# Relation rows of a graph network kernel: another split of their building over the stages

## What is computed

```python
edge_index = jnp.stack([src, dst])
x = x + _L0_gnn_ref(_layernorm(x), edge_index, ...)      # 3 mean-aggregation layers
x = x + _L0_ffn_ref(_layernorm(x)[None], ...)[0]         # 16 experts, the best 2 for each node
x = x + _L1_gnn_ref(_layernorm(x), edge_index, edge_type_500, ...)
x = x + _L1_ffn_ref(_layernorm(x)[None], ...)[0]         # 8 experts, the best 2 for each node
```

```python
h_src = h_hc[src]
r_uv = r_hc[edge_type]
m = clifford_linear(h_src * r_uv, msg_w, msg_b)
gate = jax.nn.sigmoid(r_uv.reshape(r_uv.shape[0], -1) @ gate_w.T + gate_b)
m = m * gate[:, :, None]
```

## Time and profile before

| what | value |
| --- | --- |
| median of three executions | 3093.87 us |
| the profiled execution | 3092.59 us |
| its span, first to last instruction | 3091.0 us |
| mean granted TensorE clock | 0.915 of full speed |
| TensorE matmul busy | 2442.2 us (79%) |
| VectorE busy | 1786.1 us (58%) |
| GpSimd busy | 1742.3 us (56%) |
| ScalarE busy | 1450.7 us (47%) |
| moved by DMA | 516.56 MB, 167 GB/s in the mean |

### The profile page before, as it was taken

How to read it: one execution, slowest core, us unless ns; L and a number is a source line. 1 busy time by engine, 2 the same in 40 slices (tenths; PEclk the granted TensorE clock), 3 DMA queues, 4 the chain that set the end, 5 groups by cost and what they waited for, 6 DMA issues and landing times. The chain is left out here.

```text
span 3091.0 us, 52879 instructions
## 1 busy us (share of the span) xinstructions
PE 2442.2 (79%) x14195; PEld 1910.2 (62%) x14195; DVE 1786.1 (58%) x5132; ACT 1450.7 (47%) x3766; POOL 1742.3 (56%) x1702
## 2 busy tenths in 40 slices
PE   1759999969999489850877777787877775899997
PEld 0336666747777478750655555555555554799996
DVE  7669889747788521037776666666666666311110
ACT  0357666535565333333644444444444433455553
POOL 1647777667774045422777777777777750233332
PEclk9989999989999589985998999988898987899998
DMA  6748777578886233543666666666666643443232
GB/s 226 253 143 233 227 209 211 168 227 257 263 251 186 85 109 103 168 128 125 197 186 185 180 186 184 182 182 187 181 187 185 190 119 101 121 106 77 49 65 64
DMA packets 289373, 516.56 MB, mean 167 GB/s; under 512 B 79344, under 2 KB 137057, under 8 KB 287084
## 3 DMA queue, kind: packets, MB, share of 16 engines
q0 software_dynamic: 86192, 225.20, 28.2%
q1 hardware_dynamic: 185532, 267.85, 26.4%
q10 hardware_dynamic: 17392, 20.46, 2.0%
HBM read 381.08 MB, written 137.11 MB: 168 GB/s over the span
## 5 line engine op out<-in xcount | busy, mean ns | idle before, releaser
L726 POOL DMA_INDIRECT agg_r_rows<-h_table,parts_and_x x832 | 831.0, 999 | 336.9 <-issue 230.1
L817 PE MATMUL agg_r_sums<-agg_r_rows,agg_r_onehot 128*128 128x257 f32 x1664 | 489.4, 422 | 259.9 <-DVE agg_r_rows L798 171.8
L817 PEld LDWEIGHTS agg_r_sums<-agg_r_rows,agg_r_onehot 128*128 128x128 f32 x1664 | 305.4, 203 | 396.3 <-issue 318.0
L686 ACT ACTIVATE agg_r_gap<-iota,parts_and_x 128x128 f32<-128x128 f32 x832 | 286.6, 392 | 449.8 <-PE agg_r_sums L817 419.8
L780 DVE TENSOR_TENSOR acc<-acc,agg_r_sums 128x257 f32 (+1 forms) x834 | 351.9, 422 | 129.1 <-PE agg_r_sums L817 44.9
L1723 POOL DMA_INDIRECT rl_buf<-r_table,kinds x304 | 327.6, 1078 | 150.0 <-issue 78.9
L2119 PEld LDWEIGHTS f_pH<-f_xT,f_w 128*128 128x128 f32 x2816 | 332.3, 195 | 40.0 <-ACT f_xT L2197 17.9
L2119 PE MATMUL f_pH<-f_xT,f_w 128*128 128x128 f32 x2816 | 346.7, 280 | 9.9 <-ACT f_xT L2197 4.5
L831 PE MATMUL agg_r_spread<-xn 128*128 128x257 bf16 x2664 | 350.2, 292 | 0.0
L1526 PE MATMUL la_acc<-la_parts,la_counts 128*128 128x512 f32 x1250 | 309.1, 404 | 29.3 <-DVE la_parts L1633 29.3
L2138 PE MATMUL f_pY<-f_w,f_hT 128*128 128x256 f32 x1408 | 325.6, 381 | 7.5 <-DMA f_w<-in_L_ffn_w 7.5
(11 more groups left out here) (418 smaller groups left out, 3596.8 us busy)
## 6 DMA issues: line engine op xcount, KB each, us to landing
agg_r_rel<-relation_rows SPq DMA_DIRECT2D x305, 260.0 KB, 3.0
relation_rows<-rl_buf SPq DMA_DIRECT2D x152, 260.0 KB
relation_rows<-rm_buf SPq DMA_DIRECT2D x125, 260.0 KB, 3.3
agg_r_rows<-h_table,parts_and_x POOLq DMA_INDIRECT x832, 3.2
f_w<-in_L_ffn_W SPq DMA_DIRECT2D x18, 512.0 KB, 5.4
f_w<-in_L_ffn_W SPq DMA_DIRECT2D x9, 1024.0 KB, 4.8
f_w<-in_L_ffn_w SPq DMA_DIRECT2D x30, 256.0 KB, 3.1
f_w<-in_L_ffn_w SPq DMA_DIRECT2D x15, 512.0 KB, 3.6
```

The source lines that it names most:

```text
L686: last = nc.scalar.activation(gap[:, n % HOT, t, :], c.iota[:, 0:P], ACT.Abs, bias=c.tab["b_near"][:, column(g) + t:column(g) + t + 1])
L726: pool.indirect_dma_start(rows[:, n % SLOTS, t, :], None, table, bass.IndirectOffsetOnAxis(ap=indices[:, t:t + 1], axis=0)).then_inc(s_row ...
L817: last = nc.tensor.matmul(sums[:, (2 * n + t) % BANKS, 0:used], onehot[:, n % HOT, t, :], rows[:, n % SLOTS, t, 0:used], start=True, stop= ...
```

## The change

28, 152 and 125 pairs become 18, 136, 135 and 16 pairs. The last 16 are new beside the first router's scoring: `norm_and_gate` gets a `RelationRows` with a ring of eight pairs. There GpSimd issues the gathers of eight pairs, clears the semaphores and issues the other eight; SyncE stores two or three pairs ahead of each of the five row stores and three behind them, and waits for all. In `gnn0_start` SyncE stores four pairs, then four (before: seven), then two ahead of each product store (before: three) and none behind. All 305 pairs are built as before, and nothing else is changed.

```diff
--- before.py
+++ after.py
@@ -79,7 +79,7 @@
         ORDER.append(("extra", (_n + 1) // EXTRA_EVERY - 1))
 MADE = [n for n in range(BLOCKS) if n >= FIRST_MADE and (n - FIRST_MADE) % MADE_EVERY == 0]
 STORED = [n for n in range(BLOCKS) if n not in MADE]
-SHARES = (56, 304, 250)
+SHARES = (36, 272, 270, 32)
 assert sum(SHARES) == 2 * len(STORED) and len(ORDER) == BLOCKS + EDGES_AT // 2
 GW = 3 * D + 2
 CHUNK = 5
@@ -839,7 +839,7 @@
                     beside.tensor(pe, n)
 
 
-def norm_and_gate(nc, c, name, ne, gate, gate_bias, logits, xn_table, update=None, tables=()):
+def norm_and_gate(nc, c, name, ne, gate, gate_bias, logits, xn_table, update=None, tables=(), relation=None):
 
     PRODUCTS, LATE = 3, 2 * J
     with Core(nc) as k:
@@ -855,6 +855,7 @@
             a_turns, product = k.ps(f"{name}_a_turns", [P, 2, 512]), k.ps(f"{name}_product", [P, PRODUCTS, 512])
             s_at, s_aT, s_product, s_used = (k.sem(f"{name}_{x}") for x in ("at", "aT", "product", "used"))
         s_tables = k.sem(f"{name}_tables_in")
+        work = RelationRows(nc, c, k, f"{name}_r", *relation, ring=8) if relation else None
         with nc.Block() as block:
 
             @block.sync
@@ -862,9 +863,14 @@
                 for out, src in tables:
                     sp.dma_start(out, src).then_inc(s_tables, 16)
                 for i in range(NJ):
+                    if work:
+                        work.store(sp, work.pairs * i // (NJ + 1), work.pairs * (i + 1) // (NJ + 1))
                     sp.wait_ge(s_xn, (i + 1) * J)
                     sp.dma_start(xn_table[i * J * P:(i + 1) * J * P, :].rearrange("(t p) d -> p t d", p=P), c.xn[:, i * J:(i + 1) * J, :])\
                         .then_inc(s_table, 16)
+                if work:
+                    work.store(sp, work.pairs * NJ // (NJ + 1), work.pairs)
+                    work.stored(sp)
                 sp.wait_ge(s_table, 16 * NJ)
                 if tables:
                     sp.wait_ge(s_tables, 16 * len(tables))
@@ -988,7 +994,11 @@
 
             @block.gpsimd
             def _(pool):
+                if work:
+                    work.fetch(pool, 0, work.RING)
                 Core.clear(pool)
+                if work:
+                    work.fetch(pool, work.RING, work.pairs)
 
 
 def row(ap):
@@ -1174,7 +1184,7 @@
                     sp.dma_start(out, src, allow_slow_non_contiguous=True).then_inc(s_more[q // 6], 16)
                 work.store(sp, 0, 4)
                 eb.save_starts(sp)
-                work.store(sp, 4, 11)
+                work.store(sp, 4, 8)
                 sp.wait_ge(s_norm, NT)
                 sp.dma_start(z[:, D:2 * D].rearrange("(t p) d -> p t d", p=P), h[:, :, :]).then_inc(s_saved, 16)
                 sp.wait_ge(s_w, 4)
@@ -1182,7 +1192,7 @@
                     sp.dma_start(folded[l - 1, :, 0:4 * D], f.w[:, l, :, :].rearrange("p k n -> p (k n)")).then_inc(s_saved, 16)
                     sp.dma_start(folded[l - 1, :, 4 * D:5 * D], f.shift[:, l, :]).then_inc(s_saved, 16)
                 for b in range(NJ):
-                    work.store(sp, 11 + 3 * b, 14 + 3 * b)
+                    work.store(sp, 8 + 2 * b, 10 + 2 * b)
                     sp.wait_ge(s_z0, (b + 1) * J)
                     sp.dma_start(z[b * J * P:(b + 1) * J * P, 0:D].rearrange("(t p) d -> p t d", p=P), f.z[:, b * J:(b + 1) * J, :])\
                         .then_inc(s_saved, 16)
@@ -1190,7 +1200,7 @@
                         eb.save_blocks(sp)
                     if b == 3:
                         eb.save_groups(sp)
-                work.store(sp, 11 + 3 * NJ, work.pairs)
+                work.store(sp, 8 + 2 * NJ, work.pairs)
                 sp.wait_ge(s_saved, 16 * (5 + NJ))
                 work.stored(sp)
                 eb.saved(sp)
@@ -2784,7 +2794,8 @@
         xn_table = c.dram("xn_table", [NP, D])
         norm_and_gate(nc, c, "ng0", E0, *c.gates[0], logits[0], xn_table, None,
                       [(c.tab[n][:, :], c.tab[n + "_d"]) for n in ("b_src", "b_near", "b_start")]
-                      + [(c.tab["b_tile"][:, 2 * LAG:HALVES + 2 * LAG], c.tab["b_tile_d"])])
+                      + [(c.tab["b_tile"][:, 2 * LAG:HALVES + 2 * LAG], c.tab["b_tile_d"])],
+                      (r_table, relation_rows, sum(SHARES[:3]), SHARES[3]))
 
         c.h = c.sb("h1", [P, NT, D])
         c.h_rstd, c.h_down = c.sb("h1_rstd", [P, NT]), c.sb("h1_down", [P, NT])
```

## The result

The kernel after takes 3070.38 us in the median of four executions (3063.36 to 3073.00), the kernel before on the same chip 3096.91 (3089.11 to 3101.50): ratio 0.9922, 95% interval 0.9905 to 0.9940. Its profiled execution took 3068.61 us with a span of 3067.0.

A forecast was written before the change was run, and what follows sets the result against it. Relation rows were taken to end the first dense product and count matrix, arithmetic layers 1 and 2. The terms -8.7 - 16.5 + 4.9 + 9.5 = -10.8 us gave 3083 us, with an 8-in-10 range of 3075 to 3090.

The forecast's parts named there:

- What bounds the kernel: Relation rows end the first dense product and count matrix (some 17 us late); arithmetic ends layers 1 and 2, leaving about 25 us free.
- 5.42 us: Time from the end of the last store's issue to the next stage's first instruction, taken from the count matrix's end.
- First dense product: 10 pairs fewer there: next stage's first instruction at 158.4 against 167.12, -8.7 us (ends -8, -10).
- 5.14 + 1.5: First dense product's end: 5.14 us behind the last issue as before, plus 1.5 for a 640 KB transfer's slower landing.
- Count matrix: 16 pairs fewer there: the last tile's issue plus 5.42 us ends the stage, -16.5 us (ends -15, -18).
- Layers 1 and 2: 10 pairs more there: 20 gathers cost 25.2 us, stage ends at 1011.3 against 1006.4, +4.9 us (ends +1, +7).
- The cover of 25 us is just used up: Layers 1 and 2: added gathers fill the free time, so nearly all the price is one gather, store and landing.
- Scoring: 16 new pairs beside the first router's scoring: 50.4 us against 40.88, +9.5 us (ends +8, +12).
- Cheap tails: Rival: layers' extra pairs end with the arithmetic (+1), scoring's tail is short (+8); -16.2 us, 3077.7; chance 0.14.
- Held gathers: Rival: in the scoring, 6.1 us of VectorE's work hold GpSimd's gathers; sum -4.7 us, 3089.2; chance 0.16.
- Slower: Rival: scoring's gathers 1.78 us apart, adding 16.1 us; +5.3 us, 3099; sign changes at spacing 1.61; chance 0.06.

## Why the prediction was wrong

**What bounds the kernel** was read rightly: the relation rows ended the first two stages, and moving them gained there.

**The step that failed** is "So a barrier alone costs 0.3 us, while a stage whose last act is a store costs more", with 5.42 us taken from the earlier trace rows as the price behind a last store. I used it at three ends, and at all three it was about 3 us too dear: 2.53 us behind the last tile (count matrix), 2.0 us to SyncE's readiness and 0.3 for the release (layers), 2.64 us from the last issue (1025.40) to the experts' first instruction (scoring). In the earlier trace rows 3.4 of the 5.42 us were SyncE waiting for GpSimd, which the first instruction of the next stage can't show and the barrier's rows can. The bracket [8.87 <-POOLq L1253] in the earlier trace rows had the figure in plain sight: GpSimd's idle time ahead of its next gather, most of it its own DRAIN.

- *First dense product, -8.7 forecast, -9.0 measured (-8.8 in the means).* Right in size, with two errors that nearly cancel. The store was issued 0.56 us later than I said; from its end to the count matrix's first instruction it took 5.83 us, not 5.14 + 1.5. Of these SyncE's landing is 3.0 (ready at 155.3), and about 2.5 go between the release at 155.6 and the first instruction at 158.12: I had taken them for landing, and they are there in both versions (164.2 to 167.12 before); ahead of that instruction GpSimd's list clears the semaphores. Before, of the 5.14 us only 1.9 were SyncE's landing (161.98 to 163.9).
- *Count matrix, -16.5 forecast, -21.0 measured (-20.2 in the means).* The tail behind the last tile's issue went from 21.96 to 2.53 us, 2.9 short of the forecast for it. The other 1.5 us are the stage's body, 464.3 us against 462.7; in the other three profiles with 272 tiles it was 463.1 to 464.8, so that is the spread and no effect.
- *Layers 1 and 2, +4.9 forecast, +0.06 measured.* The gathers cost what I said: the last one starts 346.5 us into the stage and not 321.4, 25.1 us for 20 of them. "The cover of 25 us is just used up" held too. Then I added the tail of 5.42 us, of which 2.3 exist: 3.1 of the 4.8 us by which I missed. The other 1.7 are a second term: from the last gather's start to the end of its pair's issue I had kept the 5.89 us of before, and it took 4.14 (969.90 to 974.04).
- *Scoring, +9.5 forecast, +7.75 measured.* The last gather starts 39.7 us into the stage (40.5 forecast), its issue ends 6.28 later (4.5 forecast, though 5.89 stood in the rows), and the tail is 2.64, not 5.42.

The misses are -0.3, -4.5, -4.8 and -1.8, together -11.4 us of the four stages. Of these 2.9, 3.1 and 2.8, together 8.8 us, are the one tail used with the same sign three times. The rest are small terms: the body of the count matrix, which is spread, and the time from the last gather to its pair's issue, 1.7 too long in the layers and 1.8 too short in the scoring, where the last gather started 0.8 us sooner than I had summed. My range treated doubts about the tail as if they would cancel.

**The rivals.** *Cheap tails* was the nearest (layers +1 and scoring +8 forecast, +0.06 and +7.75 measured), but I applied it to the additions alone; the same tail ends the count matrix, and with it there the sum is -16.2 - 3 = -19 us, against -22.2 measured. *Held gathers* fell: 0.95 us each with 0.30 between them and none over 970 ns, in all three profiles with 32 tiles beside the scoring. The rule of the Trainium skill (GPSIMD Engine Reference, Key points), by which GpSimd collides with VectorE instructions that have two SBUF inputs, has no effect that this stage's trace shows: VectorE's operations with two inputs take 0.15 to 0.17 us there, the last one 0.57, and none of the 32 gathers was lengthened. That the scaling operations of the earlier trace rows were in a 2-port mode, which the prediction's "agrees" takes for granted, no row shows. *Slower* fell with it, since its spacing of 1.61 us was not reached (1.26).

**What I had said the profile would show:** right for the count matrix's first instruction (about 158), for the pairs behind the last tile, for 32 gathers 1.26 us apart and for the last relation issue in the layers (350.7 against 352); the mark for a covered addition, VectorE's last operation followed within 4 us by the tables of the scoring, came true (975.90 to 979.41, 3.5 us). Wrong: 5.7 us from the last tile's issue on (2.9), and a scoring of 50 us (48.6).

**What stays open.** What GpSimd's DRAIN waits for isn't shown; no run changes it. Its end lies 8.5 to 9.1 us behind the start of the last gather in all seven profiles with 304 tiles beside the count matrix, 8.0 with 288, 6.2 to 7.5 with 272 or 280; 5.1 to 7.7 in the layers and the scoring, 4.3 to 7.3 in the first dense product. It isn't the last rows under way: at the end of the count matrix before, SyncE issues the last store, which waits for the last gather's rows, at 647.6, and from 649.3 us to the release the core's DMA queues move no packet at all, while the DRAIN goes on to 653.1.

## What to carry to other kernels

Split the work that fills idle queues until gathers, stores and arithmetic of each stage end together: up to that bend a tile is free (272 to 288 beside the matrix), beyond it each costs its whole gather, 1.26 us (16 tiles cost 20 us beside the matrix and 20.9 beside the layers). Before a tail is priced, read the rows of the barrier itself, with every engine's DRAIN and the moment at which each queue is ready: the gap from the last issue to the next stage belongs to whichever is last, and it changes owner when work moves. A price that is used several times with one sign makes one doubt, not several, and the range has to carry it whole.

## What was unexpected of the hardware

GpSimd isn't through with its list when the line of its last gather ends. The Trainium skill (Perfetto Trace Analysis, DMA Instruction — SWDGE (GPSIMD)) says that the profile's end of such an instruction is the end of descriptor generation and not of the data's movement. The trace agrees: at the end of the count matrix before, the last gather's line ends at 645.18, GpSimd's DMA queue still moves packets behind 646.8, and the store that waits for the gather's rows is issued at 647.6. But the DRAIN lasts longer than both: it ends 4.3 to 9.1 us behind the start of that 0.95 us line, while a 260 KB store of SyncE has landed 1.7 to 2.0 us behind its last issue. In the scoring of the kernel before, which has no gather, GpSimd's DRAIN takes 0.05 us. Where the gathers end only just ahead of the stores, as at the count matrix's end before, the DRAIN behind the last gather thus ends the stage 3.4 us behind the last store, even though the store waits for that gather.
